# Graph attention with residual norm: four target tiles' weighted sum formed transposed, one Exp and a min per weight, sums started while x loads

## What is computed

```python
h        = x @ W_sa
s_left   = h @ a_sa[0, :512];  s_right = h @ a_sa[0, 512:]
e        = where(adj != 0, exp(-leaky_relu(s_left[:, None] + s_right[None, :], 0.01)), 0)
x_a      = (e / (sum(e, axis=1) + 1e-5)) @ h
x_b      = adj @ (x @ W_gcnb) + b_gcnb
gate_a   = sigmoid([adj @ x, x] @ Wa.T + ba);  gate_b = sigmoid([adj @ x, x] @ Wb.T + bb)
out      = layernorm(x + sigmoid(gate_a * x_a + gate_b * x_b))
```

## Time and profile before

| | |
|---|---|
| Median of 3 runs | 1010.31 us |
| Span of the profiled execution | 1010.0 us |
| PE busy | 970.0 us (96%) |
| DVE busy | 817.8 us (81%) |
| ACT busy | 586.9 us (58%) |
| POOL busy | 143.4 us (14%) |
| DMA | 67.74 MB, 67 GB/s over the span |

### The profile page before, as it was taken

How to read it: one execution, slowest core, us unless ns; L and a number is a source line. 1 busy time by engine, 2 the same in 40 slices (tenths; PEclk the granted TensorE clock), 3 DMA queues, 4 the chain that set the end, 5 groups by cost and what they waited for, 6 DMA issues and landing times.

```text
span 1010.0 us, 15242 instructions
## 1 busy us (share of the span) xinstructions
PE 970.0 (96%) x4358; PEld 796.7 (79%) x4358; DVE 817.8 (81%) x1474; ACT 586.9 (58%) x1691; POOL 143.4 (14%) x373
## 2 busy tenths in 40 slices
PE   6777999999999999999999999999999999999996
PEld 3556788888888888888888888888888888888885
DVE  6989979779777877977977887797797797788476
ACT  4635757566645755665665565566565566457341
POOL 5533010011011011001101101101110110110111
PEclk8889999999999999999999999999999999999999
DMA  7753211210221121121021122112102102211220
GB/s 234 217 163 105 65 49 35 78 57 22 76 67 46 43 78 45 33 78 57 21 78 57 33 66 70 52 34 78 57 21 78 57 21 78 64 41 51 79 79 21
DMA packets 36163, 67.74 MB, mean 67 GB/s; under 512 B 4400, under 2 KB 6960, under 8 KB 36144
## 3 DMA queue, kind: packets, MB, share of 16 engines
q1 hardware_dynamic: 36144, 67.52, 22.1%
HBM read 60.69 MB, written 6.82 MB: 67 GB/s over the span
## 4 chain that ended last, share of the span: by engine, by line
PE 85%; DVE 8%; issue 4%; DMA 1%; ACT 0%; SPq 0%; POOL 0%; DVEq 0%; POOLq 0%; ACTq 0%
PE z L546 14%; PE z L547 14%; PE z L573 14%; PE z L575 14%; PE z L574 14%; PE proj L608 13%; DVE product L674 2%; PE zt L596 2%; DVE e_raw L746 1%; DVE e_lo L754 1%; DVE e_hi L750 1%; DMA adj<-adj_t_dram 1%; DVE adj_r L220 1%; DVE esums L751 1%; DMA work<-x_dram 1%
## 5 line engine op out<-in xcount | busy, mean ns | idle before, releaser
L546 PE MATMUL z<-x_hi,adj_r 128*128 128x512 f32 x676 | 274.6, 406 | 13.4 <-DVE x_lo L692 10.8
L573 PE MATMUL z<-x_hi,e_hi 128*128 128x512 f32 x676 | 265.8, 393 | 13.6 <-DVE e_lo L754 13.4
L547 PE MATMUL z<-x_lo,adj_r 128*128 128x512 f32 x676 | 267.8, 396 | 0.0
L434 ACT ACTIVATE e_raw<-l_row,r_col 128x128 f32<-128x128 f32 x676 | 214.5, 391 | 88.5 <-DVE e_lo L754 88.3
L575 PE MATMUL z<-x_hi,e_lo 128*128 128x512 f32 x676 | 264.4, 391 | 0.0
L574 PE MATMUL z<-x_lo,e_hi 128*128 128x512 f32 x676 | 264.4, 391 | 0.0
L439 ACT ACTIVATE e_raw<-e_raw,r_neg 128x128 f32<-128x128 f32 x676 | 215.3, 391 | 5.1
L447 ACT CAST adj_r<-adj 128x640 fp32r<-128x640 f32 x144 | 93.7, 651 | 200.1 <-DMA adj<-adj_t_dram 143.0
L746 DVE SCALAR_TENSOR_TENSOR e_raw<-adj,e_raw 128x512 f32<-128x512 f32 x155 | 113.5, 732 | 115.9 <-ACT adj_r L447 109.0
L751 DVE TENSOR_REDUCE esums<-e_raw 128x128 f32<-128x640 f32 x156 | 179.4, 1150 | 0.0
L573 PEld LDWEIGHTS z<-x_hi,e_hi 128*128 128x128 f32 x676 | 127.6, 189 | 43.8 <-DVE e_lo L754 17.1
(11 more groups left out here) (104 smaller groups left out, 830.4 us busy)
## 6 DMA issues: line engine op xcount, KB each, us to landing
adj<-adj_t_dram SPq DMA_DIRECT2D x108, 256.0 KB, 2.8
adj<-adj_t_dram SPq DMA_DIRECT2D x53, 320.0 KB, 3.0
out_dram<-work SPq DMA_DIRECT2D x25, 256.0 KB, 2.0
work<-x_dram SPq DMA_DIRECT2D x14, 256.0 KB, 3.6
adj<-adj_t_dram SPq DMA_DIRECT2D x16, 192.0 KB, 3.9
w_gate<-x_dram SPq DMA_DIRECT2D x12, 256.0 KB, 3.7
work<-w_sa_dram SPq DMA_DIRECT2D x4, 256.0 KB, 4.7
work<-w_gcnb_dram SPq DMA_DIRECT2D x4, 256.0 KB, 3.1
```

The source lines that it names most:

```text
L434: ins = nc.scalar.activation(e[:, k, :], l_row[:, parity, :], ACT.Relu, bias=r_col[:, j + k:j + k + 1])
L546: nc.tensor.matmul(z2[parity][:, :], buffer[:, k, :], x_hi[:, jt, :], start=(jt == 0), stop=False)
L547: ins = nc.tensor.matmul(z2[parity][:, :], buffer[:, k, :], x_lo[:, jt, :], start=False, stop=(jt == TILES - 1))
L573: nc.tensor.matmul(z1[parity][:, :], e_hi[s][:, k, :], x_hi[:, jt, :], start=(jt == 0), stop=False)
```

## The change

The kernel body is written anew; what is computed is the same. Nothing is a hardware loop any more.

- z1 of four target tiles (a block; 7 blocks, the last of 2 tiles) is formed transposed: x_hi/x_lo chunks of 128x128 are stationary, e of one source tile and four target tiles (128x512) moves, into four PSUM banks. A step is one source tile of one block, 182 steps in all. z2 stays as it was, and runs two target tiles ahead of the projections (`phases`: a quarter of a block, 6 or 7 steps, carries z2 of tile t+2 and the projections of tile t).
- Weights: with the scores negated, u = exp(0.99 * (l + r)) by one Exp of 128x512, min(mask, u), then times exp(0.01/0.99 * r') per source. The row's own factor cancels against the denominator and stays in the 1e-5 term.
- The sum of e over sources is a running sum on DVE (`esum`), one instruction per step.
- z1 needs no transposes. The two projections no longer share a bank's sum: ACT scales the first (`scale_p1`), DVE adds the second scaled (`add_p2`).
- The adjacency is loaded twice: as [source, 4 targets] for the mask (512-byte pieces, `load_adj`) and as [target, 4 sources] for z2 (2048-byte pieces, `load_raw`).
- Block 0's z1 runs while x still loads, one step per arriving source tile. All rests are DVE's; 8 matmuls on ones run first.

```diff
@@ PE
-            def chunk_z1(t, parity, c):
-                j, n = CHUNKS[c]
-                s = c % RING
-                pe.wait_ge(e_lo_ready, t * NC + (c + 1))
...
+            def sum_z1(g):
+                b, j = divmod(g, TILES)
+                s, n = g % E_RING, cols(b)
+                pe.wait_ge(e_lo_ready, g + 1)
+                for k in range(KT):
+                    if j == 0 and b > 0:
+                        pe.wait_ge(z1_copied, KT * (b - 1) + k + 1)
+                    kk = slice(k * P, (k + 1) * P)
+                    nc.tensor.matmul(z1[k][:, 0:n], x_hi[:, j, kk], e_hi[s][:, 0:n], start=(j == 0), stop=False)
+                    nc.tensor.matmul(z1[k][:, 0:n], x_lo[:, j, kk], e_hi[s][:, 0:n], start=False, stop=False)
+                    ins = nc.tensor.matmul(z1[k][:, 0:n], x_hi[:, j, kk], e_lo[s][:, 0:n], start=False,
+                                           stop=(j == TILES - 1))
+                ins.then_inc(e_used, 1)
...
+            for m in range(1, 4):
+                sum_z2(m)
+            for j in range(TILES):
+                if j == TILES - 2:
+                    sum_e(0)
+                sum_z1(j)
+                if j % 2 == 0 and 4 <= j // 2 + 2 < 2 * CHUNKS:
+                    sum_z2(j // 2 + 2)
...
+            for b, q, t in phases():
+                for i, j in enumerate(QUARTERS[q]):
+                    if i == 0:
+                        since(pe, zt_lo_ready, 2 * t)
+                        if q == 0:
+                            pe.wait_ge(denoms, b)
+                        turn(t, turned)
+                    for c in quarter_chunks(q, i):
+                        sum_z2(chunk_number(t + 2, c))
+                    if j == TILES - 2:
+                        sum_e(b)
+                    sum_z1(b * TILES + j)
+                    if i == 1 and t >= 1:
+                        project_z2(t - 1)
+                    if i == 4:
+                        project_z1(t)
...
+            project_z2(LAST - 2)
+            pe.wait_ge(denoms, BLOCKS)
+            turn(LAST - 1, turned)
+            turn(LAST, z2[0])
+            pe.wait_ge(u_ready, LAST - 1)
...
@@ ACT
-                for k in range(n):
-                    ins = nc.scalar.activation(e[:, k, :], l_row[:, parity, :], ACT.Relu,
-                                                bias=r_col[:, j + k:j + k + 1])
...
+            def steep(g):
...
+                since(act, e_lo_ready, g - U_RING + 1)
+                nc.scalar.activation(u[g % U_RING][:, 0:cols(b)], l_row[:, 0:cols(b)], ACT.Exp,
+                                     bias=r_col[:, j:j + 1]).then_inc(exp_done, 1)
+            def weights_hi(g):
...
+                since(act, e_used, g - E_RING + 1)
+                nc.scalar.activation(e_hi[g % E_RING][:, 0:cols(b)], u[g % U_RING][:, 0:cols(b)], ACT.Copy,
+                                     scale=c_col[:, j:j + 1]).then_inc(e_hi_ready, 1)
+            def adjacency(m):
...
+                since(act, adj_r_used, m - ADJ_R_RING + 1)
...
+            for b, q, t in phases():
+                for i, j in enumerate(QUARTERS[q]):
+                    g = b * TILES + j
+                    steep(g + 1)
+                    if j == TILES - 2 and b < LASTB:
+                        load_l(b + 1)
+                    weights_hi(g)
+                    for c in quarter_chunks(q, i):
+                        adjacency(chunk_number(t + 2, c))
+                    if i == 0 and t >= 1:
+                        act.wait_ge(proj_done, 2 * t - 1)
+                        scale_p1(t - 1, proj)
+                        z2_hi(t - 1)
+                    if i == 1:
+                        if q == 0:
+                            copy_z1(b - 1)
+                        gate_exps(t)
+                    if i == 2:
+                        copy_z2(t + 1)
+                    if i == 3:
+                        z1_hi(t)
...
@@ DVE
-                nc.vector.tensor_reduce(esum[:, c, :], e.rearrange("p j i -> p i j"), AX_X, ALU.add) \
...
+            def weights(g):
...
+                nc.vector.scalar_tensor_tensor(w, adj[g % ADJ_RING][:, 0:width(b), :].rearrange("p t i -> p (t i)"), 0.0,
+                                               w, ALU.not_equal, ALU.min).then_inc(masked, 1)
...
+                    nc.vector.scalar_tensor_tensor(esum[:, 0:n], w, c, esum[:, 0:n], ALU.mult, ALU.add) \
+                        .then_inc(esum_steps, 1)
+                dve.wait_ge(e_hi_ready, g + 1)
+                nc.vector.scalar_tensor_tensor(e_lo[s][:, 0:n], w, c, e_hi[s][:, 0:n].bitcast(F32), ALU.mult,
+                                               ALU.subtract).then_inc(e_lo_ready, 1)
...
+            for i in range(WIDE, LOOK):
+                source(i)
+            for j in range(TILES):
+                weights(j)
+                if j + LOOK < PIECES:
+                    source(j + LOOK)
...
+                    if i == 0:
+                        if t >= 1:
+                            z2_lo(t - 1)
+                        if q == 0:
+                            denominators(b - 1)
+                    if i == 1:
+                        if t >= 1:
+                            add_bias(t - 1)
+                        if t >= 2:
+                            normalise(t - 2)
+                    if i == 2:
+                        gate_parts(t + 1)
+                        make_gates(t)
+                    if i == 3:
+                        z1_lo(t)
+                        if EARLY_L <= t + 9 < TILES:
+                            left_joined(t + 9, t + 1)
+                    if i == 4:
+                        if t >= 1:
+                            add_p2(t - 1, proj)
+                        gate_dots(t + 1)
+                    if i == 5 and t >= 1:
+                        residual(t - 1)
```

More of the change, by code:

```diff
@@ L348, in _ @@
[L348 to L357 removed]
+            load_piece(0)
@@ new lines, in z2_hi, with tanh_half, copy_v @@
+            def z2_hi(t):
+                act.wait_ge(turn_done, t + 1)
+                act.wait_ge(proj_done, 2 * t + 1)
+                nc.scalar.copy(zt_hi[:, :, :].rearrange("p k i -> p (k i)"), turned[:, :]).then_inc(zt_hi_ready, 1)
+            def tanh_half(t):
+                act.wait_ge(u_ready, t + 1)
+                nc.scalar.activation(y[:, t % 2, :], y[:, t % 2, :], ACT.Tanh, scale=0.5).then_inc(tanh_ready, 1)
+            def copy_v(h, v):
+                act.wait_ge(v_summed, KT * (h + 1))
+                nc.scalar.mul(v[:, :], bank[6 + h][:, :], -STEEP).then_inc(v_ready, 1)
@@ new lines, in _ @@
+            act.wait_ge(proj_done, 2 * (LAST - 2) + 1)
+            scale_p1(LAST - 2, proj)
+            z2_hi(LAST - 2)
+            act.wait_ge(e_used, STEPS)
+            for k in range(KT):
+                nc.scalar.copy(last_z1(k)[0], z1[k][:, 0:2 * P]).then_inc(z1_hi_ready, 1)
+            copy_z2(LAST)
+            gate_exps(LAST - 1)
+            act.wait_ge(turn_done, LAST)
+            act.wait_ge(proj_done, 2 * (LAST - 2) + 2)
+            nc.scalar.copy(zt_hi[:, :, :].rearrange("p k i -> p (k i)"), turned[:, :]).then_inc(zt_hi_ready, 1)
@@ L526, in _ @@
+            gate_exps(LAST)
+            tanh_half(LAST - 2)
+            act.wait_ge(turn_done, LAST + 1)
+            nc.scalar.copy(adj_r[0][:, :, :].rearrange("p k i -> p (k i)"), z2[0][:, :]).then_inc(zt_hi_ready, 1)
+            act.wait_ge(proj_done, 2 * (LAST - 1) + 1)
+            scale_p1(LAST - 1, proj)
+            tanh_half(LAST - 1)
+            act.wait_ge(proj_done, 2 * LAST + 1)
+            scale_p1(LAST, bank[5])
+            tanh_half(LAST)
         @block.tensor
@@ new lines, in _ @@
+            pe.wait_ge(ones_ready, 1)
+            for _ in range(WARM):
+                nc.tensor.matmul(z2[1][:, 0:P], ones, ones, start=True, stop=True)
+            sum_v()
+            sum_z2(0)
+            spread_l()
+            for m in range(1, 4):
+                sum_z2(m)
+            for j in range(TILES):
+                if j == TILES - 2:
[3 more added lines that the diff above has]
+                    sum_z2(j // 2 + 2)
@@ L945, in _ @@
[L945 to L952 removed]
+            piece_lo(0)
@@ new lines, in _ @@
+            z2_lo(LAST - 2)
+            for k in range(KT):
+                dve.wait_ge(z1_hi_ready, k + 1)
+                hi, lo = last_z1(k)
+                nc.vector.tensor_tensor(lo, z1[k][:, 0:2 * P], hi.bitcast(F32), ALU.subtract).then_inc(z1_lo_ready, 1)
+            denominators(LASTB)
+            add_bias(LAST - 2)
+            gate_parts(LAST)
+            add_p2(LAST - 2, proj)
+            make_gates(LAST - 1)
+            dve.wait_ge(zt_hi_ready, 2 * LAST - 1)
+            nc.vector.tensor_tensor(zt_lo[:, :, :].rearrange("p k i -> p (k i)"), turned[:, :],
+                                    zt_hi[:, :, :].rearrange("p k i -> p (k i)").bitcast(F32),
+                                    ALU.subtract).then_inc(zt_lo_ready, 1)
@@ new lines, in _ @@
+            gate_dots(LAST)
```

(16 more changed lines are left out.)

1161 lines of the change are left out of this document (486 added, 675 removed).

## The result

| | before | after |
|---|---|---|
| Median | 1010.32 us | 1000.42 us (999.75 to 1002.06, 4 runs) |
| Ratio | 1 | 0.9905 [0.9892, 0.9917] |
| Span of the profiled execution | 1010.0 us | 998.3 us (its own time 1000.1) |
| PE busy | 970.0 us | 956.2 us |
| DVE, ACT, POOL busy | 817.8, 586.9, 143.4 us | 669.7, 440.8, 115.0 us |

A forecast was written before the change was run, and what follows sets the result against it. PE's work was taken as the bound: 929.4 us of work, 27.1 lost at the start and 13.8 at the end give 970.3, as a median 970.6 us; forecast 962 to 980, widened to 960 to 992.

The forecast's parts named there:

- the queue walk: Start: following DVE's queue in order, with z2 chunks ahead of z1's first step, put z1's start at 34.0 us.
- The 512-byte pieces: Mask loads in block 0: 0.9 us each, a step's DMA 2.0 us (1.8 to 2.7) of 3.63, so hidden.
- the rival by which the turn makes it slower: Each of 24 quarters waits 2.1 us or more at its turn: +50, 1021 us; chance 0.05.
- The back edges: Loop branches, 11 before and none after: at 2.7 us each 30 us more gained; none taken; rival 941 to 961, shared chance 0.06.
- PE is thus the slower of the two, by little: Block 0: PE needs 3.63 us every second step, against DVE's 3.45 up to j = 19 and 2.8 after.
- SP's own issues ... fit too: Block 0: SP's DMA issues, 2.5 per step at 0.4 us, fit within the step.
- it costs nothing: End of block 0: the next l row's load lands in 2.8 us, PE needs that step 6 us later, so no cost.
- nothing, up to 1.5 us for each of 6 block starts: From block 1 on: quarter turns and block-start bank copies priced at nothing, up to 1.5 us per block start.
- The end, 28.3 us: After the last z1 step: DVE's queue, projections to 17.4 us, then the last tile's chain to its store, 28.3 us.
- Start bound by DVE or DMA: Rival: block 0 steps of 3.7 to 4.1 us set by DVE, 976 to 985 us, or DMA binds; chance 0.10.
- its case for DMA: Block 0: if a mask piece costs 108 ns, the step is 4.8 us and the time 1000 us.
- Lead lost in the steady part: Rival: ACT's queued waits for PE cost 0.1 to 0.2 us in each of 156 steps, 985 to 1002 us; chance 0.13.

The follow-up runs named there:

- e1: Changed kernel with block 0's raw adjacency load issued at the head of its step, before the mask load's wait: 987.92 us, ratio 0.9765.
- e8: Changed kernel with block 0's raw adjacency load issued one step later, behind odd steps' mask loads: 1040.04 us, ratio 1.0294.
- e5: Changed kernel with the raw load early (e1), the l rows stored earlier (e2) and the end's edits (e3) together: 981.22 us, ratio 0.9698.
- e6: e5 with z2 pieces 2 and 3 put behind block 0's first and third steps instead of ahead of the first: 979.19 us, ratio 0.9688.
- e12: e6 with Exp and add_p2 reordered, gate and bias loads late, l rows stored in step 6, that store on ScalarE's queue: 976.38 us, ratio 0.9664.
- e2: Changed kernel with the l rows' store issued 10 steps earlier in block 0 and 3 steps earlier in other blocks: 996.4 us, ratio 0.986.
- e3: Changed kernel with tile 25's y in its own buffer and normalise of tiles 23 and 24 behind the next residual: 996.79 us, ratio 0.9858.
- e11: e12 with the store still on SyncE's queue, and all of x and the first two z2 before block 0's steps: 987.91 us, ratio 0.9771.

## Why the prediction was wrong

**What held.** PE's work fell as costed. The pitch of z1 with x stationary is that of the other matmuls, 9 of them here:

```profile
551.89 0.39 PE L530 MATMUL bank<-x_hi,adj_r 128*128 128x512 f32 x1
...
553.93 0.39 PE L514 MATMUL bank<-e_hi,x_lo 128*128 128x512 f32 x1
```

(553.93 - 551.89) / 9 = 0.2267 us, and 0.12 at 256 columns in the last block; the bank that changes costs nothing. z1's first matmul came within 0.1 us of the queue walk. The 512-byte pieces did not bind: the DMA share from block 1 on is 0.37, about a third as written. No quarter waits for the turn; the rival by which the turn makes it slower is out. The back edges were worth nothing, as the earlier trace rows had it: with none left, the part from block 1 on is 4.7 us longer than the work counted at the old pitches, not shorter. The Trainium skill says that a taken branch can have to wait for its target ("Runtime: NRT & Kernel Launch", "Instruction fetch mechanics"); the 30 us more that I worked out for it are in neither trace.

**The step that failed: the start, "PE is thus the slower of the two, by little", 3.63 us a step.** The sum took each engine's busy time per step and the larger of them. SP's part stands in one sentence of it, "SP's own issues ... fit too": they were counted, not placed. In SP's queue `load_raw` stands behind a wait for the mask, and in ACT's queue the copy of that piece stands in front of the next step's Exp; so a ring was closed (mask, load, 3.3 us of landing in the median, copy, Exp, mask) that no engine's busy time shows; two steps took 8.0 to 9.4 us from one such load to the next up to 108 us, where the forecast has 7.3. e1 opens it: 11.1 of the 17.9 us; e8 widens it. With the l rows stored earlier too (e5), block 1 starts at 130.06, 6.4 us over the forecast. In that trace PE's stands in block 0 add up to 4.6 us, where 1.5 were priced, and the granted clock is 0.91 from 34 to 44 us and 0.85 from 114 to 124, which by my estimate costs another 2.4. e6 and e12 come nearer (126.38 and 124.38, against 123.7) by an order of PE and of the store that the forecast did not have. DVE's step was right: 3.41 us where nothing waits, against 3.45, although an instruction with a per-partition scalar takes 0.75 us and not 0.69; ACT's take 0.72, not 0.62 (below).

**The l row, "it costs nothing".** The landing was read from a 256 KB load of 2048-byte rows, 2.8 us, and the store in front of it had no term at all. The store took 11.2 us and delayed the loads around it, the l row's among them: 6.4 us here, 4.1 in e2, where the store had landed long before. So 2.8 was not far off for the load alone; the store was the missing term. In the later blocks, priced at "nothing, up to 1.5 us for each of 6 block starts", this is most of the 4.7 us that were missing: e2's stretch is 819.8 long, 1.5 over the forecast.

**The end, 28.3 us.** Its chain followed one tile. DVE's queue holds three, and `normalise` waits there for the moments of the tile before; a wait for a free y was not looked for. The miss is 5.4 us; e3 gets 4.0 of them back.

**The rivals.** "Start bound by DVE or DMA" had the right place and the wrong cause, and its 976 to 985 for DVE was too good; that its case for DMA gave 1000 is a coincidence, since no engine of the DMA was full (share 0.53). "Lead lost in the steady part" gave the right time by the wrong part: it wanted 0.1 to 0.2 us in each of 156 steps, and all of them together lost 4.7. With the three repairs of e5 the kernel runs at 981.22, still 10.6 us over the sum; e6, with an order of PE that is not the forecast's, gives 979.19 and e12 976.38. So the forecast priced nearly what the change could give, and not the queue order it was written in.

**Open.** Why loads behind the 4-byte store land late. e12's stretch from 124.38 to the last z1 step is 819.8, 1.5 us over the forecast, in no gap over 0.4 us. What 4-byte stores in the later blocks cost after e2's edit was not tried by itself, nor a form of the l row without them.

## What to carry to other kernels

Where a step's engines are all below full, write down for each transfer which wait stands ahead of its issue in the issuing queue, and for each instruction that waits for it what stands behind: the ring of the two can set the pace, and not the busiest engine, as it did in block 0 here. A load must be issued ahead of waits for the step that is running, and a copy with slack should not stand in front of a chain without. Give a transfer the landing time of its own pattern: a 2 KB store in 4-byte pieces took 7.4 to 12.4 us where a load of 256 KB takes 2.9, and the loads issued behind it landed late, whichever of two queues had issued the store.

## What the runs showed of the hardware

- The 4-byte store (512 pieces, 2 KB) took 7.4 to 12.4 us to land over all traces, in block 0 and later, and 256 KB loads issued in the 3 us after it 8.3 to 12.4 us instead of 2.9, wherever it stood and whichever queue issued it. PE lost nothing by it in the later blocks of e2; in block 0 its stand behind the store was 0.7 us (e5) to 10.1 us (e11). The Trainium skill, "DMA: Bandwidth & Descriptors", section "Specifications", says that transfers below 512 bytes make the DMA read, modify and write; no run here tells whether that is the cause.
- On 512 columns a VectorE instruction with a per-partition scalar takes 0.07 us longer than one without, and a ScalarE one some 0.1 us longer than a cast (L344) or a Tanh (L401) without (groups by form; busy, mean ns):

```profile
L674 DVE SCALAR_TENSOR_TENSOR e_lo<-u,c_col,e_hi 128x512 fp32r<-128x512 f32 x156 | 117.3, 752 | 52.9 <-ACT e_hi L337 45.7
...
L662 DVE SCALAR_TENSOR_TENSOR u<-adj,u 128x512 f32<-128x512 f32 x156 | 107.0, 686 | 0.0
```

```profile
L329 ACT ACTIVATE u<-l_row,r_col 128x512 f32<-128x512 f32 x156 | 112.7, 722 | 38.0 <-DVE e_lo L674 19.9 <-DMA l_row<-l_rows 18.1
...
L344 ACT CAST adj_r<-raw 128x512 fp32r<-128x512 f32 x156 | 95.4, 611 | 118.0 <-PE bank L531 97.7 <-DMA raw<-adj_t_dram 20.3
...
L401 ACT ACTIVATE y<-y 128x512 f32<-128x512 f32 x26 | 16.3, 627 | 4.4 <-DVE y L748 4.4
```

- Short stands of PE can cost its clock. After the one of 1.3 us at 412.7, with only eight matmuls of one column behind it until 414.92 and hundreds of microseconds without a gap before, the granted clock from 416 to 420 us is 0.57 in the mean, mostly the lower of the two levels of 1.2 and 2.4 GHz (0.50 and 1.00); after e12's one of 2.5 us at 61.4 it stayed at 1.00 from 66 to 84.

```profile
412.00:416.00 4.00, 2.66 (x17) 2.05 (x16) 3.32 (x6) 3.33 (x6) 0.00 (x0) 1.00 0.35 87
416.00:420.00 4.00, 4.00 (x12) 3.13 (x11) 3.24 (x6) 0.72 (x1) 2.11 (x5) 0.57 0.46 159
```
